# Attention and FFN layer on 8 cores: large transfers issued from ScalarE's queue, casting loads cut into pieces

## The reference

```python
qkv = einsum('btc,fc->btf', x, w_qkv)                 # 16 heads of 64
p = softplus(q @ k.T * hs**-0.5) ** 2 * causal
out = (p / (p.sum(-1, keepdims=True) + 1e-9)) @ v
x = layernorm(x + out @ w_proj.T + b_proj)
Wq = clip(round(W / s), -128, 127) * s                # s = max|W| / 127, for both FFN weights
h = gelu(x @ Wfc_q.T + b_fc + 2 * (x @ A_fc.T) @ B_fc.T)
x = layernorm(x + h @ Wproj_q.T + b_proj + 2 * (h @ A_proj.T) @ B_proj.T)
# x: 16 x 2048 x 1024, so 2 sequences a core; FFN width 4096, LoRA rank 16
```

## Time and profile before

| | us |
|---|---|
| median of 3 runs | 2141.54 (2138.22 to 2186.15) |
| the profiled execution | 2140.47 |
| span of its slowest core (core 3) | 2138.9 |
| spans of the 8 cores | 2126.6 to 2138.9 |
| PE busy, whole span | 1929.6 (90%) |
| DVE, ACT, POOL busy | 1042.4, 855.0, 448.2 |
| mean granted TensorE clock | 0.964 of full speed |

### The profile page before, as it was taken

How to read it: one execution, slowest core, us unless ns; L and a number is a source line. 1 busy time by engine, 2 the same in 40 slices (tenths; PEclk the granted TensorE clock), 3 DMA queues, 4 the chain that set the end, 5 groups by cost and what they waited for, 6 DMA issues and landing times.

```text
span 2138.9 us, 26841 instructions; the slowest of 8 cores (2126.6 to 2138.9 us)
## 1 busy us (share of the span) xinstructions
PE 1929.6 (90%) x8834; PEld 759.0 (35%) x8834; DVE 1042.4 (49%) x1613; ACT 855.0 (40%) x1026; POOL 448.2 (21%) x515
## 2 busy tenths in 40 slices
PE   6897987888987899999867889999999999999998
PEld 2332332222322333322222234444444444444443
DVE  2675887766689777788759731111110101020202
ACT  2464765765422466677533421212222121313130
POOL 1121221221156412222225421111010101010201
PEclk9998998999999999999978999999999999999999
DMA  8656554357466443344485465020202111110101
GB/s 130 149 135 146 155 150 131 100 128 149 122 188 181 131 112 116 114 124 128 125 222 163 133 191 169 30 69 30 70 30 59 40 50 50 50 60 20 60 10 49
DMA packets 118023, 228.35 MB, mean 107 GB/s; under 512 B 59282, under 2 KB 59538, under 8 KB 115186
## 3 DMA queue, kind: packets, MB, share of 16 engines
q1 hardware_dynamic: 109042, 195.03, 30.2%
q0 software_dynamic: 8848, 31.63, 8.7%
HBM read 182.21 MB, written 58.98 MB: 113 GB/s over the span
## 4 chain that ended last, share of the span: by engine, by line
PE 72%; DVE 10%; DMA 8%; issue 6%; POOL 2%; ACT 2%; SPq 0%; DVEq 0%; POOLq 0%; ACTq 0%
PE ps_s L924 20%; PE ps_a L976 10%; PE ps_f L976 10%; PE ps_a L718 8%; PE ps_f L341 8%; PE ps_s L674 6%; PE ps_f L365 5%; DVE a_ph L700 3%; DMA a_bc<-recscr 3%; PE ps_f L616 3%; DVE a_QO L776 2%; DMA recscr<-g_rec 2%; PE ps_f L497 2%; DMA g_den<-a_nd 1%; ACT a_ph L685 1%
## 5 line engine op out<-in xcount | busy, mean ns | idle before, releaser
L685 ACT ACTIVATE a_ph<-ps_s 128x1024 bf16<-128x1024 f32 (+1 forms) x576 | 560.7, 976 | 506.8 <-PE ps_s L674 505.4
L931 ACT ACTIVATE b_h<-ps_s,g_bfc,g_scl 128x512 bf16<-128x512 f32 x256 | 199.1, 778 | 649.1 <-PE ps_s L924 649.1
L924 PE MATMUL ps_s<-b_xT,b_Wfc 128*128 128x512 bf16 x2048 | 444.0, 379 | 0.0
L718 PE MATMUL ps_a<-a_ph,a_V 128*65 128x512 bf16 (+3 forms) x1280 | 354.0, 366 | 94.4 <-DVE a_ph L700 73.5
L700 DVE TENSOR_TENSOR a_ph<-a_ph 128x1024 bf16<-128x1024 bf16 (+1 forms) x576 | 399.9, 719 | 24.9 <-ACT a_ph L685 12.8
L341 PE MATMUL ps_f<-a_xT,a_wqk 128*128 128x512 bf16 x1024 | 307.5, 396 | 35.5 <-DMA a_xT<-xT 16.9
L692 POOL TENSOR_TENSOR a_ph<-a_ph,g_mask 128x256 bf16<-128x256 bf16 x256 | 196.4, 785 | 498.6 <-ACT a_ph L685 497.7
L981 DVE SCALAR_TENSOR_TENSOR g_x<-ps_a,g_scl,g_x 128x512 f32<-128x512 f32 x32 | 24.0, 751 | 566.1 <-PE ps_a L976 566.1
L924 PEld LDWEIGHTS ps_s<-b_xT,b_Wfc 128*128 128x128 bf16 x2048 | 200.4, 98 | 241.6 <-issue 0.2
L674 PE MATMUL ps_s<-a_QO,a_K 64*128 64x512 bf16 (+3 forms) x1280 | 226.3, 367 | 2.6 <-ACT a_QO L351 2.5
L976 PE MATMUL ps_a<-b_Wp,b_h 128*128 128x512 bf16 x1024 | 224.4, 379 | 0.0
(11 more groups left out here) (47 smaller groups left out, 937.1 us busy)
## 6 DMA issues: line engine op xcount, KB each, us to landing
a_w<-wfc SPq DMA_DIRECT2D x64, 512.0 KB, 5.7
a_w<-wpF SPq DMA_DIRECT2D x64, 512.0 KB, 4.5
a_bc<-recscr SPq DMA_DIRECT2D x64, 256.0 KB, 4.4
g_x<-x SPq DMA_DIRECT2D x32, 512.0 KB, 4.0
x1scr<-g_x SPq DMA_DIRECT2D x32, 512.0 KB, 4.0
g_x<-x1scr SPq DMA_DIRECT2D x32, 512.0 KB, 3.2
out<-g_x SPq DMA_DIRECT2D x32, 512.0 KB, 2.6
a_wqk<-wqk POOLq DMA_DIRECT2D x16, 512.0 KB, 7.4
```

What stands on the lines that cost most here:

```text
L685: s_read[sl] = P.op("scalar", lambda E: E.activation(dst, src, AF.Softplus, scale=HS ** -0.5), waits=[tok, ph_av[q]])
L718: tok = P.op("tensor", lambda E, c0=c0, n=n, off=off, x0=x0, hd=hd, fin=fin: E.matmul(ps_a[0:65, hd * 512 + c0: hd * 512 + c0 + n], V4[:, ...
L924: tok = P.op("tensor", lambda E, cc=cc, c0=c0: E.matmul(ps, b_Wfc[:, c0:c0 + 128], b_xT[:, (g % 2) * 4096 + cc * 512:(g % 2) * 4096 + (cc ...
L931: h_tok[(g, f)] = P.op("scalar", lambda E: E.activation(b_h[:, f * 512:(f + 1) * 512], ps, AF.Gelu, bias=g_bfc[:, f:f + 1], scale=g_scl[:, ...
```

## The change

Four things change; what is computed does not, and PE and DVE have the same instructions in the same order as before.

1. **Large transfers go to ACT's queue.** The `a_w` loads from the fourth on, the stores of rounded weights, x loads and x1 stores of the attention stage, the bias, all `b_Wfc` loads and three `b_Wp` loads: 270 DMAs. SP keeps 277: the division's small ones, the first three `a_w` loads, four `b_Wp` loads, the transposes, and what the FFN stage needs.
2. **Casting loads in pieces.** `in_parts` cuts a load of POOL's into 4, 8 or 16 column pieces, one every few ticks; whoever needs the load waits for the last piece.
3. **Places.** Weight stores 3 ticks after their data instead of 2, `a_w` loads of the rounding stage too; the x1 store of a tile one tick after its scaling instead of at once (but that of tile 31 at once); x load n + 2 half a projection later.
4. In the first window the pieces of the v weights come ahead of those of the q and k weights.

```diff
+        def in_parts(sem, dst, src, n, step, after):
+            c = dst.shape[1] // n
+            end = sem.n + 16 * n
+            def part(i):
+                P.dma("gpsimd", sem, lambda E: E.dma_start(
+                    out=dst[:, i * c:(i + 1) * c], in_=src[:, i * c:(i + 1) * c]),
+                    waits=after if i == 0 else ())
+            part(0)
+            for i in range(1, n):
+                if step:
+                    after_ticks(i * step, lambda i=i: part(i))
...
+            return (sem, end)
...
-            k_wo.append(P.dma("gpsimd", msem("wo"), lambda E: E.dma_start(out=a_wo[:, :], in_=d_wo)))
+            k_wo.append(in_parts(msem("wo"), a_wo[:, :], d_wo, 16, 4, ()))
...
-            w_tok[k] = P.dma("sync", msem(f"w{sl}"), lambda E: E.dma_start(
+            w_tok[k] = P.dma("sync" if k < 3 else "scalar", msem(f"w{sl}"), lambda E: E.dma_start(
...
-            after_ticks(2, lambda: w_load(k + 2))
+            after_ticks(2 if k < 69 else 3, lambda: w_load(k + 2))
...
-                    wb_st[sl] = P.dma("sync", msem(f"wb{sl}"), lambda E: E.dma_start(
+                    wb_st[sl] = P.dma("scalar", msem(f"wb{sl}"), lambda E: E.dma_start(
...
-                after_ticks(2, store)
+                after_ticks(3, store)
...
+            if n >= 4:
+                to_store[n - 4]()
...
-            x_dma[n] = P.dma("sync", msem(f"x{sl}"), lambda E: E.dma_start(
+            x_dma[n] = P.dma("scalar" if n < NT else "sync", msem(f"x{sl}"), lambda E: E.dma_start(
...
-            st = P.dma("sync", msem(f"st{sl}"), lambda E: E.dma_start(
-                out=dst[t * 128:(t + 1) * 128, :], in_=x), waits=[ta])
...
+            def store():
+                if n in stored:
+                    return
+                st = P.dma("scalar" if n < NT else "sync", msem(f"st{sl}"), lambda E: E.dma_start(
+                    out=dst[t * 128:(t + 1) * 128, :], in_=x), waits=[ta])
...
+            to_store[n] = store
+            if n < NT - 1:
+                after_ticks(1, store)
+            else:
+                store()
...
-                x_load(n + 2)
...
+                        x_load(n + 2)
...
-                    load_wqk(2, after=[qk_pe[0]]), load_wv(0, 1, after=[v_pe[(0, 0)]]))))
+                    load_wv(0, 1, after=[v_pe[(0, 0)]], n=4, step=1), load_wqk(2, after=[qk_pe[0]], n=4, step=4))))
...
-                load_wqk(gp + 2, after=[qk_pe[gp]])
+                load_wqk(gp + 2, after=[qk_pe[gp]], n=4, step=5)
...
-            wfc_tok[fb] = P.dma("sync", msem(f"wfc{fb}"), lambda E: E.dma_start(
+            wfc_tok[fb] = P.dma("scalar", msem(f"wfc{fb}"), lambda E: E.dma_start(
```

More of the change, by code:

```diff
@@ L229, in build_program, with load_wqk, load_wv, load_xT @@
         k_xT = {}
[L231 to L242 removed]
+        def in_parts(sem, dst, src, n, step, after):
[10 more added lines that the diff above has]
+                else:
+                    part(i)
+            return (sem, end)
+        def load_wqk(gp, after=(), n=1, step=0):
+            pr, sl = gp % NP, gp % 2
+            k_wqk[gp] = in_parts(
+                msem(f"wqk{sl}"), a_wqk[:, sl * 2048:(sl + 1) * 2048], d_wqk[pr, :, :], n, step, after)
+        def load_wv(s, hf, after=(), n=1, step=0):
+            k_wv[(s, hf)] = in_parts(msem("wv"), a_wv[:, :], d_wv[hf, :, :], n, step, after)
+        def load_xT(s, tg, after=(), n=1, step=0):
+            k_xT[(s, tg)] = in_parts(
+                msem(f"xT{tg}"), a_xT[:, tg * 4096:(tg + 1) * 4096], d_xT[s, tg, :, :], n, step, after)
         load_wqk(0)
@@ L819, in window @@
                             main.append(ch_do(("ldx", tg), lambda tg=tg: load_xT(
-                                1, tg, after=[xT_pe[(0, tg)]])))
+                                1, tg, after=[xT_pe[(0, tg)]], n=4, step=2)))
             if pr in (1, 2, 3):
@@ L845, in first_loads @@
             if gp >= 1 and gp + 2 < SEQ * NP:
[L846 removed]
+                load_wqk(gp + 2, after=[qk_pe[gp]], n=4, step=5)
             if gp == 4:
[L848 removed]
+                load_wv(1, 0, after=[v_pe[(0, 1)]], n=8, step=4)
             if gp == 8:
[L850 removed]
+                load_wv(1, 1, after=[v_pe[(1, 0)]], n=8, step=4)
         def ffn_loads():
```

31 lines of the change are left out of this document (12 added, 19 removed).

## The result

The changed kernel is slower: 1.031 times the kernel before, interval 1.027 to 1.035. It took 2209.7 and 2207.3 us, the kernel before 2141.5 us at the median, so the loss is 67 us.

What follows compares the result with a forecast made beforehand. PE idles 200 us in the first 1267 us, with DVE waiting for late small DMAs. A gain of 65 us less costs of 8.6, 10.5, 9 and 3 us gives -34 us: 2107 us, range 2070 to 2150 us.

Steps and rivals of the forecast that it cites:

- The gain of 65 us: Nine PE gaps behind late small DMAs: 85% of 76.6 us comes back, 49 us idle and 16 us clock.
- Rival C: Small DMAs stay late because all queues share the engines: 2172 us with nothing gained, 2139 us with half; chance 0.25.
- the sum: Gain and costs together: -65 + 8.6 + 10.5 + 9 + 3 = -34 us, giving 2107 us.
- The sign I named: In the changed profile, `a_bc` lands below its 4.4 us; if not, rival C, by which small DMAs stay late.
- Last piece of pair 2: Start of window 1, near 117 us: PE waits 6.9 us for the weights, 8.6 us with clock.
- Store of tile 31: FFN, block 18: the store on ACT holds up gelus; PE waits 8.5 us, 10.5 us with clock.
- Issue time on ACT: First 1267 us: 270 issues make 28 softplus or evictions late by 0.8 us; 9 us reach PE.
- the 25 that I had set as a mark: New waits of DVE for softplus of over 25 us would speak for a larger issue cost.
- Chunks, 3 us: Weight chunks go out at their tick on ACT, later than on SP: 3 us more on PE.
- Projections, nothing: x loads on ACT wait 4.0 us for x1 stores to land; that fits into two ticks, no cost.
- Rival D: ACT held by x1 store landings, decisive once a hold exceeds two ticks: 2197 us if all reaches PE; chance 0.07.
- The clock: Before the FFN: a granted clock that stays at 0.94 would say that the gaps only changed places.

Runs made afterwards that it cites:

- run 5: None of the kernel's work: one small transfer issued alone or after a large load; a large load costs the put 2.5 us on its own queue, 1.9 us on ACT's.
- run 14: Kernel before with `a_wo` alone loaded in 16 pieces, other casting loads whole, no queue changed: 0.9958.
- run 16: Kernel before with only the `a_wqk` loads of pair 3 and later in four pieces, five steps apart: 1.0032.
- run 12: Kernel before with `a_w` loads and `a_wb` stores on ACT's queue, after one step in place of two: 1.0061.
- run 4: Changed kernel with the x1 store of tile 31 alone back on SyncE: 1.0268.
- run 13: Kernel before with only the residual's stores on ACT's queue, one step late; x loads and tile 31's store on SyncE: 1.0019.
- run 9: Kernel before with `a_w` loads and `a_wb` stores alone on ACT's queue, at the changed kernel's ticks: 1.0141.
- run 11: Kernel before with `a_w` loads (from the 70th) and `a_wb` stores after three steps in place of two, still on SyncE's queue: 1.0041.
- run 10: Kernel before with `a_w` loads and `a_wb` stores on ACT's queue, both after two steps as in the kernel before: 1.0084.
- run 8: Kernel before with x loads and residual stores alone on ACT's queue, at the changed kernel's places, tile 31's store too: 1.0112.
- run 1: Kernel before with all casting loads in pieces, no queue changed: 1.0009, 2150 us.

## Why the prediction was wrong, step by step

- **The gain of 65 us: this step failed.** I wrote that the bytes ahead of the small transfers go away when they go to another queue. Beside a load of another queue the put lands almost as late as behind one of its own (run 5): leaving the queue gives 0.6 us to a put and nothing to a fetch. DVE's waits for `a_bc` and `g_den`, which were to fall from 75 to under 15 us, are 87.7 us. What the change did win is `a_wo` in pieces, 9 us (run 14), and `a_wqk`'s pieces took most of that again (run 16). Rival C had the reason right, but I gave it a quarter and let its price end at no gain. That the move could be a loss by itself stood nowhere in the sum; run 12 shows one of 0.6% with the places all but undone.
- **The sign I named misled.** `a_bc`'s median landing was to fall below 4.4 us, and it did, to 3.9. The put before it in the chain went from 1.7 to 3.4 us. One link of a chain shows nothing about the chain.
- **Last piece of pair 2: right.** PE's wait for it is 5.6 us; the sum had 6.9. The 1.7 us of clock behind it were not taken apart.
- **Store of tile 31: right, in mechanism and size.** PE stands 9.9 us, the sum had 8.5, and ACT waits 14.8 us for L607. Taking it back gave 9 us with its clock (run 4), the sum had 10.5; the intervals leave that size open, the wait in the trace doesn't.
- **Issue time on ACT, 9 us: not isolated.** DVE's waits for a softplus went from 12.8 to 26.9 us, just past the 25 that I had set as a mark, but part of that is ACT standing for landings. With the stores alone on ACT, 31 more issues, the cost was 0.2% (run 13). I had taken ACT's waits for DVE at nothing, as for work three ticks old; the residual stores follow their scaling after one tick, and ACT stood 33.7 us for it there, at little cost.
- **Chunks, 3 us: mis-sized by ten.** Chunks and `a_wb` stores on ACT cost 1.41%, 30 us (run 9): 9 for the late place (run 11), 18 for the queue (run 10), the two nearly additive. I had looked for DVE's wait for chunks alone, 19.5 us before and 24.5 in the changed kernel, and had no term for the landings of the `a_wb` stores. In run 9 DVE's waits for the division grew by 25.1 us, those for `a_wb` by 12.3 and those for chunks by 5.9.
- **Projections, nothing: failed.** I compared a landing of 4.0 us with two ticks of 2.2 us. Landings there were up to 16.2 us. ACT stood at least 88 us for them in 13 waits (43.4, 39.9 and one of 4.8 us), and PE 32.3 us for a softplus. Rival D described this, with the right place and the right condition (a landing beside other transfers), and I gave it 0.07. Its price, all 90.5 us, was too high: by itself the mechanism costs some 11 us (run 13 against run 8), a size within the noise of the two. In the changed kernel x on ACT is worth 1.0312/1.0164, 1.5% or 31 us with tile 31's store.
- **The clock: the sign was right, the scale was not in the sum.** I took clock as a share of the long gaps. In pairs 9 to 13 seven waits of DVE for DMAs, none over 3.3 us, went with 9.6 us of clock beside 4.4 us of idle time. Which short waits lower the clock, and whether it is these, no run shows.
- **The sum.** In place of -34 us: +30 chunks and stores of weights, +24 x and residual (9 of them tile 31's), +2 all pieces (run 1), which is 56 of the 67 us. The 11 us left may come only when all parts are together, or be noise: the three intervals leave as much open. The later load of x and the new order of the loads in the first window were not varied by themselves.

## What to carry to other kernels

Before a large transfer is moved to another engine's queue, ask whether the old queue's order kept it away from small transfers with a consumer waiting: here the move saved a small transfer at most 0.6 us, and it gave up that order. What helped is fewer bytes under way when the small one is issued: cut the one very large load, leave the middling ones whole, and send large loads right behind a small one that is already on its way. Judge it by the waits and the time, not by a median landing: the put's rose to 3.0 us in run 1 at no net cost. And a DMA issue with a wait for a landing belongs on a queue whose engine computes nothing; price it by the longest landing beside other traffic, not by the median.

## What the hardware showed that I had not expected

- A 4 KB put that lands in 1.4 us alone takes 3.9 us behind a 512 KB load of its own queue and 3.3 us beside one of another queue; as 16 pieces of 256 bytes in place of 128 of 32 bytes it takes 3.2 us in both cases. The same page of the Trainium skill, section "Queues, rings and completion order", has each engine going round its queue rows packet by packet; I had read from it that a small transfer in a row of its own hardly waits. The rows show that this is worth 0.6 us of 2.5.
- In the trace of the kernel before, the 64 fetches of `g_den` sorted by how many large transfers were under way at their issue landed in 2.05 us (none), 2.7 us (one), 4.5 us (two) and 10.9 us (four) on average (23, 22, 16 and 3 fetches; the large ones were on SyncE's and POOL's queues). The number is not all: of those with two, one beside casting loads of 512 KB and 1 MB took 13.6 us, others 2 us.
- Issuing a DMA transpose held SyncE for 13.6 us at the longest before and 21.5 us in the changed kernel, with medians of 4.7 and 4.1 us; what stands behind it in the queue goes out only after it.
- In the quiet stretch seven DMA waits of DVE of at most 3.3 us went with a granted clock of 0.96 in place of 0.99, and the clock cost twice what the added idle time did (9.6 and 4.4 us).
